# Writing out the round loops of VectorE, ScalarE and TensorE in the convolutions and the attention gather of a graph transformer

## The reference, cut to what matters

```python
def gine_conv(x, edge_index, w1, b1, w2, b2):        # twice, in layer 0
    src, dst = (edge_index[0], edge_index[1])
    msg = jax.nn.relu(x[src])
    agg = jax.ops.segment_sum(msg, dst, num_segments=x.shape[0])
    ...

def _L1_gnn_ref(h, W, Wl, Wr, b, edge_index):        # graph attention, in layer 1
    ...
    e = el[src] + er[dst]
    e = jnp.exp(jax.nn.leaky_relu(e, negative_slope=0.2))
    rowsum = jax.ops.segment_sum(e, src, num_segments=N)
    w = e / jnp.maximum(rowsum, EPS)[src]
    heads = [jax.ops.segment_sum(w[:, hd:hd + 1] * x[dst], src, num_segments=N) for hd in range(H)]
    ...
```

## Time and profile before

| | us |
|---|---|
| median of 3 runs (6032.69 to 6035.34) | 6035.27 |
| the profiled execution, its own time | 6032.18 |
| its span in the profile | 6030.5 |
| `conv1`, first gather to last gather | 297.2 to 1465.3 |
| `conv2`, first gather to last gather | 1686.2 to 2849.6 |
| `gat`, first gather to last gather | 3924.2 to 5001.5 |

### The profile page before, as it was taken

One profiled execution on the slowest core, in us unless ns is written; L12 is line 12 of the kernel. 1 busy time (PEld: TensorE's weight loads), 2 busy tenths in 40 slices (PEclk: granted clock), 3 DMA queues, 4 the chain that ended last, 5 costly groups with the idle time before them and its releaser, 6 DMA issues. The chain is left out here.

```text
span 6030.5 us, 75495 instructions
## 1 busy us (share of the span) xinstructions
PE 3346.5 (55%) x13479; PEld 2417.9 (40%) x13480; DVE 2750.8 (46%) x6682; ACT 2082.8 (35%) x5020; POOL 3748.8 (62%) x3707
## 2 busy tenths in 40 slices
PE   4355555555646666665834753056666664229990
PEld 1144444344434444443723752034444443216660
DVE  6655555532234444443544353555555557402223
ACT  4433333332333333332311310055555554313331
POOL 4266666666766666665777777777777773530006
PEclk7577777777967777777977987578888885569995
DMA  2233333333133333334211211011111115241114
GB/s 73 91 96 93 94 94 94 92 96 70 39 84 101 99 100 100 101 99 84 36 18 10 46 31 14 4 27 27 27 27 27 27 27 116 83 161 55 56 55 131
DMA packets 280618, 407.59 MB, mean 68 GB/s; under 512 B 93991, under 2 KB 197765, under 8 KB 280262
## 3 DMA queue, kind: packets, MB, share of 16 engines
q0 software_dynamic: 142720, 275.10, 19.7%
q1 hardware_dynamic: 137798, 131.50, 7.1%
HBM read 323.82 MB, written 81.61 MB: 67 GB/s over the span
## 5 line engine op out<-in xcount | busy, mean ns | idle before, releaser
L1156 PE MATMUL conv_ps<-conv_msg,conv_S 128*128 128x256 f32 x3328 | 1202.6, 536 | 991.6 <-DMA conv_msg<-relu_xn_table,GI 521.4
L1156 PEld LDWEIGHTS conv_ps<-conv_msg,conv_S 128*128 128x128 f32 x3328 | 907.0, 281 | 1314.5 <-issue 1121.2
L1128 DVE TENSOR_TENSOR ACC<-ACC,conv_ps 128x256 f32 x1664 | 700.9, 421 | 1190.0 <-PE conv_ps L1156 1082.6
L683 POOL DMA_INDIRECT edges_by_src<-packed,rank_i x800 | 953.9, 1192 | 308.9 <-issue 240.9
L1079 POOL DMA_INDIRECT conv_msg<-relu_xn_table,GI x832 | 800.4, 962 | 430.3 <-issue 235.3
L1079 POOL DMA_INDIRECT conv_msg<-conv_table,GI x832 | 788.2, 947 | 380.0 <-issue 233.9
L1852 POOL DMA_INDIRECT gat_msg<-attn_table,GI x832 | 824.9, 992 | 266.6 <-issue 253.3
L1099 ACT ACTIVATE conv_S<-iota_row,LOC 128x128 f32<-128x128 f32 x1664 | 507.9, 388 | 890.9 <-PE conv_ps L1156 806.2
L1905 PE MATMUL gat_ps<-gat_M,gat_S 128*128 128x260 f32 x1664 | 600.1, 509 | 373.9 <-DVE ACC L1959 223.4
L1905 PEld LDWEIGHTS gat_ps<-gat_M,gat_S 128*128 128x128 f32 x1664 | 378.6, 247 | 519.5 <-issue 463.1
L2508 POOL DMA_INDIRECT combine_y<-expert_out,combine_at x98 | 94.2, 961 | 578.5 <-ACTq L2496 557.2
(11 more groups left out here) (428 smaller groups left out, 5116.8 us busy)
## 6 DMA issues: line engine op xcount, KB each, us to landing
expert_in<-heads_zrow SPq DMA_DIRECT2D x53, 256.0 KB
experts_xe<-expert_in SPq DMA_DIRECT2D x106, 128.0 KB
expert_out<-experts_y SPq DMA_DIRECT2D x106, 128.0 KB, 1.7
conv_msg<-relu_xn_table,GI POOLq DMA_INDIRECT x832, 2.7
conv_msg<-conv_table,GI POOLq DMA_INDIRECT x832, 2.7
gat_msg<-attn_table,GI POOLq DMA_INDIRECT x832
edges_by_src<-packed,rank_i POOLq DMA_INDIRECT x800, 3.1
relu_xn_table<-begin_rx SPq DMA_DIRECT2D x49, 128.0 KB, 1.7
```

The source lines that it names most:

```text
L683: pool.indirect_dma_start(edges, bass.IndirectOffsetOnAxis(ap=m.rank_i[:, j:j + 1], axis=0), m.packed[:, j:j + 1], None).then_inc(sent[g % ...
L1128: nc.vector.tensor_tensor(acc, acc, ps[k % NB][:, 0:D], ALU.add).then_inc(added, 1)
L1156: nc.tensor.matmul(ps[k % NB][:, 0:D], S[:, h % 2, k, :], msg[:, h * RING + k, :], start=True, stop=True).then_inc(summed, 1)
```

## The change

The loops `Fori` in `in_rounds` (conv) and `staggered` (gat) become loops of Python, so that the programs of VectorE, ScalarE and TensorE are written out over all 104 rounds; r is then a plain number in each of them, and all waits compare with constants. In both stages the semaphores `turns_v`, `turns_t` and `turns_a` are not allocated, and `held` does nothing when it gets None for them. The work of a round, its order and its buffers stay. SP's loop in `conv2` keeps its own semaphore, and POOL's programs are not touched.

```diff
 def held(eng, turns):
 
-    eng.sem_inc(turns, 1)
+    if turns is not None:
+        eng.sem_inc(turns, 1)
...
-        tv, tt, ta = (st.sem(n) for n in ("turns_v", "turns_t", "turns_a"))
+        tv = tt = ta = None
         ts = st.sem("turns_s")
...
-            beside = CHUNKS // DEEP if rank_sources else TILES // 2
-            four(0)
-            with eng.Fori(1, beside - 1 if rank_sources else beside) as q:
-                four(q)
-            if rank_sources:
-                four(beside - 1)
-            else:
-                four(beside, keyed=2)
-                beside += 1
-            if beside < ROUNDS // DEEP - 1:
-                with eng.Fori(beside, ROUNDS // DEEP - 1) as q:
-                    four(q, False, 0)
-            four(ROUNDS // DEEP - 1, False, 0)
+            for q in range(ROUNDS // DEEP):
+                if rank_sources:
+                    four(q, ranked=q < CHUNKS // DEEP)
+                else:
+                    four(q, keyed=4 if q < TILES // 2 else 2 if q == TILES // 2 else 0)
...
-        tv, tt, ta = (st.sem(n) for n in ("turns_v", "turns_t", "turns_a"))
+        tv = tt = ta = None
...
         def staggered(eng, step):
 
-            for r in range(-DEEP, DEEP):
-                step(r, r % DEEP)
-            with eng.Fori(1, ROUNDS // DEEP - 1) as q:
-                for h in range(DEEP):
-                    step(q * DEEP + h, h)
-            for r in range(ROUNDS - DEEP, ROUNDS):
+            for r in range(-DEEP, ROUNDS):
                 step(r, r % DEEP)
```

## The result

The changed kernel takes 6057.4 us (median of 5 runs, 6052.5 to 6061.1), the kernel before 6033.9 beside it. The ratio is 1.0038 with an interval of 1.0023 to 1.0052: slower by 0.4%. The profiled execution took 6055.1 us, with a span of 6053.4 against 6030.5.

The account below looks back on a forecast made before the run. POOL alone was taken to set the length of all three stages; 28 - 3 + 2 - 1 = +26 us on 6032.2 gave 6058, and with 3.1 us for the runs' median 6060 us, range 6022 to 6076.

Parts of the forecast that it names:

- second rival: In gat, a later first multiplication lets the fourth gather escape; rounds 10.27 us, some 6017 us in all; chance 0.10.
- The rule of the hit: In gat, a POOL gather starting inside a VectorE multiplication with both inputs in SBUF runs longer, by 0.33 to 0.43 us.
- Part 1: In gat, multiplications come 0.29 us earlier and prolong two gathers a round, not one: +28 us, bounds +20 to +34.
- Part 2: In the convolutions, shifted VectorE operations prolong other gathers, partly hidden by landing waits: -3 us for conv1, +2 for conv2.
- Part 3: Dropped increments, registers and branches hide behind waits, extra instruction fetch taken as 0; stage ends save 1 us in all.

Follow-up runs that it names:

- pad_b: Changed kernel plus two empty semaphore increments a round on VectorE, ahead of the second and third addition in the attention gather; faster than the changed kernel by 0.4%.
- the two ties: Changed kernel, gat's multiplications waiting for landings of gathers two to five: without increments 6049.7 us (ratio to before 1.0003), with two behind each wait 5999.9 us (0.9948).
- pad_a: Changed kernel plus one empty semaphore increment a round on VectorE, ahead of the second addition in the attention gather; 75 rounds of 10.75 us, 22 of 10.3.
- paced: Changed kernel with each of gat's four multiplications waiting for the landing of one of gathers two to five, no added increments; 6049.7 us, ratio to the kernel before 1.0003.
- gat_held: Changed kernel with the turn semaphores put back into the written-out attention gather, without loops or register arithmetic; 6058.7 us, ratio to the kernel before 1.0043.

## Why the prediction was right

It said 6060 us, 6022 to 6076, and slower with a chance of 0.70; measured were 6057.4. That the two lie so close is in part luck: the gather was put 6 us too high and the first convolution 3 us too low, and the recorded sum, 6058.2 + 3.1, is 6061. The reason given is the one that the runs bear out, and its second rival ("faster, by a phase on the other side") was made real by `pad_b`: it was to decide 0.16 us later and give rounds of 10.27 us, and 0.22 us later most rounds last 10.27 to 10.29.

- **The rule of the hit.** "Prolonged by (end of the multiplication - start of the gather) - 0.12 us" came from three rows. Over nine traces (those of the table, the kernel with the gather in loops, and the two ties on these chips), 1135 gathers of `gat` are over 0.97 us; 1132 of them start inside a multiplication, and for each of these the rule, with 0.13 in place of 0.12, is right to 0.015 us. The Trainium skill (SBUF — State Buffer, "SBUF: two separate sides") has the waiting side blocked until about 115 ns after the end of VectorE's instruction; an estimate by that figure makes each hit 0.24 us longer. The traces decide against it here: the hit gathers end 0.82 us after the multiplication and not 1.06, and the written-out gather lost 22 us, not 50.
- **Part 1, +28 us for the gather: +22.0 measured.** The step per round was good: the multiplication came at 2.26 us (2.25 said), the reduce moved forward from 1.35 to 1.28 us behind the round (0 to 0.09 said), the usual round became 10.65 us (10.68 said). What was mis-sized is the number of rounds. I counted all 96 of the loop; 85 of the whole stage had two hits, where 3 had them before. In most of the 13 rounds with one hit the first multiplication started 0.2 to 0.8 us later than usual, in some because the landing was late (rounds 40 and 41: reduce at 1.86 and 2.08 us), in others behind a reduce that came on time. Hence 1018 ns for the mean gather and not 1030. Late landings are no consequence of fetching: a reduce more than 1.55 us behind its round's start is seen in 4 rounds of the kernel before, in 16 of the one with the gather in loops, and in 7 of the changed one.
- **Part 2, -3 and +2 us: +0.2 and +1.5 measured.** Within the bounds. The waits for landings, 136.1 and 143.0 us, still swallow a hit on the last gather.
- **Part 3, nothing and -1 us.** In the rest of the span 0.8 us went. Instruction packets rose as longer programs need, against the earlier trace rows in the same stretch of 400 to 1100 us:

```profile
q14 instruction: 26, 0.21, 0.1%
q8 instruction: 9, 0.15, 0.1%
```

POOL's issue gaps are unchanged at 253.2 us. The Trainium skill (Runtime: NRT & Kernel Launch, "Instruction fetch mechanics") has a taken branch out of the current window stall for a fetch, which writing the loops out would save. No such gain shows here: the three stages became 23.7 us longer together.
- **A sign that was read too simply.** I had said that TensorE's waits for DMAs would grow in the convolutions. By name they fell (521.4 to 288.5 us); only the sum of its idle time, 991.6 to 1004.2, grew.

## What to carry to other kernels

Where one engine issues all gathers and never waits, the others cost it nothing by how long they work but by where they stand when a gather starts. Look at the maximum beside the median of its instructions, and at what runs at the start of each long one, before shortening an engine that waits. Look also at whether this holds on every chip: on two of the chips here POOL waited some 400 us in `gat`, and the hits didn't matter. If two such engines keep the same beat, fix their distance with a wait on the other's progress and check on which side of the edge it lands: here 0.1 us decided over 0.4 us a round.

## What the runs showed of the hardware

- The hit has sharp edges. In the nine traces every gather that starts from 0.044 us behind a multiplication's start on, and more than 0.17 us ahead of its end, is hit. None up to 0.028 us behind the start is; in between both occur (in `pad_a` 7 of 7 are hit at 0.04 to 0.06 us, and 0 of the 12 that start earlier). Nor is one that starts in the multiplication's last 0.13 us. Where the gather starts just behind the multiplication and escapes, the multiplication pays a little: it takes 0.72 to 0.77 us instead of 0.69 (134 cases, among them `paced` at 4486.84 and 4488.09 and `pad_b` at 4465.30).
- It goes one way, and not with every operation. 1296 multiplications that ran wholly inside a gather and began at least 0.06 us behind its start took 0.68 to 0.70 us. 1445 gathers started inside one of VectorE's adds (L1959 in the kernel before, one input in PSUM, 0.42 us), more than 0.13 us ahead of its end, and none of them took over 0.97 us.
- A semaphore increment in VectorE's program costs 0.11 us where it stands behind the end of an awaited add (first multiplication at 2.37 us in `pad_a`, 2.26 in the changed kernel), and nothing where it is issued while that add still runs (2.26 in `gat_held`).
- The kernel before had medians of 6034, 6034 and 6048 us in three comparisons, and of 6600 and 6818 us on two other chips. There POOL waited some 400 us in `gat` for buffers, and loops against written-out programs made a difference of 150 and 166 us in the convolutions, where on the first chips it made 2.
